# One 320-column maxima product, one shared output bank, centred weights, keys in three runs, and adds moved from GpSimd to VectorE

## The reference, cut to what matters

```python
x = x + layernorm(attention(layernorm(x)))
x = x + layernorm(ffn(layernorm(x)))
```

## Time and profile before

| | |
|---|---|
| median of 3 runs | 3582.44 us (3581.54 to 3588.01) |
| span of the profiled execution | 3584.1 us |
| what lies around the span in that execution | the page gives no time of its own beside the span; the span is 1.7 us above the median of the runs |
| TensorE matmuls | 3478.6 us busy (97%) |
| TensorE weight loads | 2683.5 us (75%) |
| VectorE | 2311.2 us (64%) |
| GpSimd | 2222.2 us (62%) |
| ScalarE | 1977.0 us (55%) |

### The profile page before, as it was taken

The page is one execution under the profiler, slowest core; times in us unless marked ns, Lnnn a source line. Parts: engine busy times, 40 slices in busy tenths (PEclk is TensorE's granted clock), DMA queues, the critical chain, the costliest instruction groups (busy, mean ns, idle before and its releaser), DMA issues.

```text
span 3584.1 us, 79850 instructions
## 1 busy us (share of the span) xinstructions
PE 3478.6 (97%) x29010; PEld 2683.5 (75%) x29010; DVE 2311.2 (64%) x4796; ACT 1977.0 (55%) x4132; POOL 2222.2 (62%) x3475
## 2 busy tenths in 40 slices
PE   8999999999997999999999999999999999999997
PEld 6888888888886677777777777777777777777774
DVE  5444444444434577777777777777777777777774
ACT  3222222222223567776676767777677767777674
POOL 1000000000001688889888898888988888988887
PEclk9999999999997899999999999999999999999999
DMA  6877887787777566666666666666666666666641
GB/s 176 240 224 210 228 235 221 209 236 229 216 236 172 131 147 155 147 150 155 150 152 147 153 152 151 150 148 155 154 150 146 151 153 157 149 144 151 153 117 42
DMA packets 493810, 603.94 MB, mean 169 GB/s; under 512 B 51080, under 2 KB 260120, under 8 KB 493480
## 3 DMA queue, kind: packets, MB, share of 16 engines
q1 hardware_dynamic: 413512, 564.80, 61.9%
q10 hardware_dynamic: 79680, 34.70, 5.4%
q0 software_dynamic: 288, 0.08, 0.0%
HBM read 361.59 MB, written 203.23 MB: 158 GB/s over the span
## 4 chain that ended last, share of the span: by engine, by line
PE 41%; POOL 17%; ACT 4%; issue 3%; ACTq 2%; DVE 1%; DMA 1%; POOLq 0%; SPq 0%; DVEq 0%
PE ps_misc L1118 11%; PE ps_sc L1049 5%; PE ps_ml L1025 4%; PE ps_mg L1030 4%; PE ps_o L1077 3%; PE ps_sc L1063 3%; PE ps_s L1096 3%; PE ps_o L1102 3%; POOL qk L809 3%; PE ps_s L1090 2%; POOL qk L812 2%; POOL qk L806 2%; ACTq L892 2%; POOL xb L842 2%; POOL ot_lo L827 2%
## 5 line engine op out<-in xcount | busy, mean ns | idle before, releaser
L937 DVE TENSOR_REDUCE mx<-ps_ml 128x2 f32<-128x384 f32 x1024 | 559.5, 546 | 334.5 <-PE ps_ml L1025 327.3
L499 PE MATMUL po<-ht_hi,w_both 128*128 128x512 f32 x2048 | 639.3, 391 | 1.6 <-ACT ht_hi L290 1.5
L897 ACT ACTIVATE ps_ml<-mask 128x384 f32<-128x384 bf16 x1022 | 500.1, 491 | 235.0 <-issue 116.2
L869 ACT ACTIVATE qk<-ps_sc 128x384 f32<-128x384 f32 (+1 forms) x1024 | 415.6, 458 | 210.6 <-PE ps_sc L1049 209.5
L499 PEld LDWEIGHTS po<-ht_hi,w_both 128*128 128x128 f32 x2048 | 385.2, 188 | 88.6 <-issue 6.5
L940 DVE TENSOR_REDUCE mx<-ps_mg 128x2 f32<-128x256 f32 x1024 | 424.7, 415 | 2.1 <-PE ps_mg L1030 1.9
L499 PE MATMUL po<-ht_lo,w_both 128*128 128x512 f32 x1024 | 399.0, 390 | 0.0
L882 ACT ACTIVATE v<-ps_sc 128x512 f32<-128x512 f32 x512 | 302.6, 592 | 93.7 <-PE ps_sc L1063 82.6
L806 POOL TENSOR_SCALAR_AFFINE_SELECT qk<-qk 128x512 f32<-128x512 f32 (+1 forms) x512 | 298.2, 582 | 87.6 <-ACT qk L869 85.0
L809 POOL TENSOR_SCALAR_AFFINE_SELECT qk<-qk 128x512 f32<-128x512 f32 x512 | 324.9, 635 | 35.0
L858 ACT ACTIVATE xb<-xb,nmb,rsb 128x512 f32<-128x512 f32 x384 | 310.4, 809 | 53.8 <-POOL nmb L799 53.5
(11 more groups left out here) (149 smaller groups left out, 8738.6 us busy)
## 6 DMA issues: line engine op xcount, KB each, us to landing
xb<-in_L_attn_x SPq DMA_DIRECT2D x256, 256.0 KB, 5.7
w_both<-q_hi_d SPq DMA_DIRECT2D x256, 256.0 KB
ks<-k_hi_d SPq DMA_DIRECT2D x128, 288.0 KB
q_lo_d<-o_lo SPq DMA_DIRECT2D x32, 1024.0 KB, 8.6
k_lo_d<-o_lo SPq DMA_DIRECT2D x32, 1024.0 KB, 10.1
w_both<-q_lo_d SPq DMA_DIRECT2D x128, 256.0 KB
vw<-v_d SPq DMA_DIRECT2D x128, 256.0 KB, 2.9
out<-xb SPq DMA_DIRECT2D x128, 256.0 KB, 3.3
```

The lines of the kernel that those rows point to most:

```text
L499: last = nc.tensor.matmul(po[bank(o, u)][:], wa[:, k, o * P:(o + 1) * P], ha[u][:, k, :], start=start, stop=stop)
L869: nc.scalar.activation(p_loc[:, i, 2 * hp:2 * hp + 2, lo:MW], ps_sc[n % 2][:, 0:2 * MW].rearrange("p (h n) -> p h n", h=2)[:, :, lo:MW], A ...
L897: nc.scalar.activation(ps_ml[u % 2][:, :, 0:MW], mask[:].rearrange("p (o n) -> p o n", o=1).to_broadcast([P, 2, MW]), ACT.Copy).then_inc(s ...
L937: nc.vector.tensor_reduce(mx[s % 2][:, 0, heads, tile], ps_ml[u % 2][:, :, 0:MW], axis=AX.X, op=ALU.max).then_inc(ml_taken, 1)
```

## The change

1. **Maxima.** Local and global keys of a tile are made neighbours in `ks`, so one product of 320 columns replaces the 192 and the 128. For this the local keys are kept in three runs with two copies of the global keys between them (`RUNS`, `GLOB_AT`); a window of 320 columns at `WINDOW_AT[tile]` holds both. The bank pair `ps_mx` is seeded with a 320-column mask (two layouts of it), and one VectorE reduction over blocks of 64 columns replaces two. A new piece `maxc` joins the blocks with three small VectorE instructions.
2. **Shared bank.** `ps_mx` takes four banks, so `ps_o` and `ps_s` become one, `ps_os`: the products with v (`ol`), the copy out (`oc`), the sums (`sl`, `sg`), their transpose, the global product (`pvgo`) and its scaling (`ogm`) use it one after another. The sums are made in four windows in one piece.
3. **Centred weights.** The mean over the output columns is taken out of `w_out`, of the second layer's matrix and of both biases, so the outputs of both layers have zero mean. Norm and residual add become one VectorE instruction, `x1` and `za`; the norm on ScalarE, the add on GpSimd and one small GpSimd instruction go.
4. **Adds.** The overlap adds go from GpSimd to VectorE (`sadd`).
5. **Loads.** Local keys come in three DMAs instead of one, global keys and values and the bias row only where they change. v is held in three buffers by step. The input of the next chunk is loaded right behind the store of the same tile. Scores and exponentials are separate pieces of the list, and all its offsets are new (`PERIOD` 16.5).

```diff
-KROW = SPAN + NGLOB
+RUNS = ((0, 2 * WIN, 0), (2 * WIN, 6 * WIN, 4 * WIN), (6 * WIN, 9 * WIN, 10 * WIN))
+GLOB_AT = (2 * WIN, 8 * WIN)
+TILE_AT = (0, 4 * WIN, 6 * WIN, 10 * WIN, 12 * WIN)
+KROW = SPAN + 2 * NGLOB
+WINDOW_AT = (0, 2 * WIN, 6 * WIN, 8 * WIN)
+MWG = P + WIN + NGLOB
...
-                for k in range(KT):
-                    dve.wait_ge(split_hi, k + 1)
-                    nc.vector.tensor_tensor(wo_lo[:, k, :], wo[:, k, :], wo_hi[:, k, :].bitcast(F32), ALU.subtract).then_inc(split_lo, 1)
+                dve.wait_ge(spec_loaded[1], 16)
+                nc.vector.tensor_reduce(wo_sum[:], wo[:], axis=AX.X, op=ALU.add).then_inc(wo_summed, 1)
...
+                    nc.vector.tensor_reduce(m_rows[:, a:a + 1], wi[:, a, :], axis=AX.X, op=ALU.add).then_inc(m_summed, 1)
...
     def load_ones(self, act, g):
...
+        for lo, hi, at in RUNS:
+            act.dma_start(ks[ROWS_MAX:ROWS_MAX + 1, :, at:at + hi - lo].bitcast(F32),
...
     def load(self, sp, c, g):
...
-            sp.dma_start(ks[dst, :, 0:SPAN].bitcast(F32),
-                         kd[rows, :].rearrange("(h p) n -> p h n", p=DH)[:, :, pad_at:pad_at + SPAN]).then_inc(done, 16)
-            sp.dma_start(ks[dst, :, SPAN:KROW].bitcast(F32),
-                         gd[rows, :].rearrange("(h p) n -> p h n", p=DH)[:, :, glob_at:glob_at + NGLOB]).then_inc(done, 16)
+            for lo, hi, at in RUNS:
+                sp.dma_start(ks[dst, :, at:at + hi - lo].bitcast(F32),
+                             kd[rows, :].rearrange("(h p) n -> p h n", p=DH)[:, :, pad_at + lo:pad_at + hi]).then_inc(done, 16)
+            if c % CPB == 0:
+                for at in GLOB_AT:
+                    sp.dma_start(ks[dst, :, at:at + NGLOB].bitcast(F32),
+                                 gd[rows, :].rearrange("(h p) n -> p h n", p=DH)[:, :, glob_at:glob_at + NGLOB]).then_inc(done, 16)
...
-        ps_ml = [pb(f"ps_ml{b}", [P, 2, 256]) for b in range(2)]
-        ps_mg = pb("ps_mg", [P, 4, P])
+        ps_mx = [pb(f"ps_mx{b}", [P, 2, 512]) for b in range(2)]
...
-        ps_o = pb("ps_o", [P, 512])
-        ps_s = pb("ps_s", [P, 512])
+        ps_os = pb("ps_os", [P, 512])
...
(TensorE, max)
-                            last = nc.tensor.matmul(ps_ml[u % 2][:, n, 0:MW], queries[n], keys[n][:, tile * P:tile * P + MW],
+                            last = nc.tensor.matmul(ps_mx[u % 2][:, n, 0:MWG],
+                                                    qs[g][0:ROWS_MAX, 2 * pair + n, tile * P:(tile + 1) * P],
+                                                    ks[g][0:ROWS_MAX, 2 * pair + n, WINDOW_AT[tile]:WINDOW_AT[tile] + MWG],
                                                     start=False, stop=True, skip_group_check=True)
-                            last = nc.tensor.matmul(ps_mg[:, n, :], queries[n], keys[n][:, SPAN:KROW], start=True, stop=True)
...
(VectorE)
+                        nc.vector.tensor_reduce(mb[s % 2][:, heads, tile, :],
+                                                ps_mx[u % 2][:, :, 0:MWG].rearrange("p h (b n) -> p h b n", n=WIN), axis=AX.X,
+                                                op=ALU.max).then_inc(mx_taken, 1)
...
+                    if name == "maxc":
...
+                        nc.vector.tensor_reduce(dst[:, 1, :, :], two(2, 3), axis=AX.X, op=ALU.max).then_inc(glob_joined, 1)
+                        nc.vector.tensor_reduce(dst[:, 0, :, :], two(0, 7), axis=AX.X, op=ALU.max).then_inc(pair_joined, 1)
+                        dve.wait_ge(pair_joined, s + 1)
+                        nc.vector.tensor_tensor(dst[:, 0, :, :], dst[:, 0, :, :], pairs[:, :, 4::5], ALU.max).then_inc(loc_joined, 1)
+                    if name == "sadd":
+                        dve.wait_ge(loc_masked, 4 * s + i + 2)
+                        nc.vector.tensor_tensor(p_sum[:, i, :, :], p_loc[:, i, :, P:MW], p_loc[:, i + 1, :, 0:WIN], ALU.add).then_inc(s_added, 1)
...
+                        nc.vector.scalar_tensor_tensor(xb[:, i, :], yb[:, i, :], rs[0][:, i:i + 1], xb[:, i, :],
+                                                       ALU.mult, ALU.add).then_inc(x1_done, 1)
...
(TensorE, sums)
+                    if name == "sl":
+                        pe.wait_ge(o_copied, s + 1)
+                        pe.wait_ge(s_added, 3 * s + 3)
...
+                        for n, (sums, windows) in enumerate(((halves[:, 0:3, 0, :], p_loc[:, 0:3, :, WIN:P]),
+                                                             (halves[:, 0:3, 1, :], p_sum[:]),
+                                                             (ps_os[:, CHUNK - P:CHUNK], p_loc[:, 3, :, WIN:MW]),
+                                                             (ps_os[:, CHUNK - WIN:CHUNK], p_last[:]))):
```

More of the change, by code:

```diff
@@ L18 @@
 from concourse import mybir
+from collections import defaultdict
 from contextlib import ExitStack
@@ new lines, in attention_phase @@
+        STEP = {
+            "max": (-24.199, -24.541, -18.13, -16.452, -14.377, -20.916, -12.047, -10.469),
+            "maxr": (-21.658, -24.356, -16.156, -17.544, -24.046, -13.821, -14.424, -11.914),
+            "seed": (-26.179, -17.313, -14.321, -21.944, -17.917, -12.257, -11.667, -5.155),
+            "maxc": (-11.643,),
+            "mt": (-8.224,),
+            "x_mt": (-6.202,),
+            "loc": (0.725, -0.098, 1.268, 5.513, 1.373, 4.656, 9.953, 10.057),
+            "x_loc": (-1.026, 6.374, 1.546, 2.758, 2.501, 12.223, 4.157, 8.885),
+            "locm": (-3.93, 0.616, -5.376, 4.294),
+            "sadd": (11.06, 10.318, 9.79),
+            "last": (4.706,),
+            "x_last": (6.509,),
+            "lastm": (-3.272,),
+            "glob": (6.095, 12.016, 7.262, 12.082),
+            "x_glob": (11.47, 10.271, 4.491, 8.982),
+            "ol": (12.531, 13.851, 13.964),
+            "oc": (12.4,),
+            "sl": (16.483,),
+            "sg": (17.734,),
+            "sums": (18.556,),
+            "pvgo": (22.001,),
+            "rglob": (20.077,),
+            "ogm": (24.906,),
+            "rloc": (20.57,),
+            "olm": (14.394,),
+            "osum": (20.265,),
+        }
@@ L734, in attention_phase @@
+            return [it[1:] for it in items]
+        SCORED = {"mt": "x_mt", "loc": "x_loc", "last": "x_last", "glob": "x_glob", "tr": "x_tr"}
         ORDER = timeline()
-        UNITS = [(*it, hp) for it in ORDER if it[0] in ("loc", "glob", "last", "mt", "tr") for hp in range(1 + (it[0] == "loc"))]
+        UNITS = [it for it in ORDER if it[0] in SCORED]
         UNIT_AT = {u: n for n, u in enumerate(UNITS)}
-        unit = lambda s, name, i, hp=0: UNIT_AT[name, s, i, hp]
-        LAST_USE = max((("loc", 3, 1), ("last", 0, 0), ("glob", 3, 0)), key=lambda use: unit(GROUPS, *use))
+        unit = lambda s, name, i: UNIT_AT[name, s, i]
@@ L739, in attention_phase @@
+        exps = iter((SCORED[name], s, i) for name, s, i in UNITS)
+        ORDER = [next(exps) if it[0] in SCORED.values() else it for it in ORDER]
+        LAST_USE = max((("loc", 7), ("last", 0), ("glob", 3)), key=lambda use: unit(GROUPS, *use))
         MISC = [it for it in ORDER if it[0] in ("out", "ffn") and it[2] % KT == 0]
@@ L1087, in item @@
-                        for n, (sums, windows) in enumerate(parts):
+                        for tile in O_PARTS[i]:
+                            if tile < 4:
+                                pe.wait_ge(loc_masked, 4 * s + tile + 1)
+                            else:
+                                pe.wait_ge(last_masked, s + 1)
+                            for h in range(4):
+                                rows, head = slice(h * DH, (h + 1) * DH), slice(h * DH, (h + 1) * DH)
+                                if tile < 4:
+                                    x0, w = (0, P) if tile == 0 else (P * tile - WIN, MW)
+                                    last = nc.tensor.matmul(ps_os[rows, x0:x0 + w], vw[s % V_BUFS][:, tile, head], p_loc[:, tile, h, MW - w:MW],
+                                                            start=tile == 0, stop=False, skip_group_check=True)
+                                else:
+                                    last = nc.tensor.matmul(ps_os[rows, CHUNK - WIN:CHUNK], vl[s % V_BUFS][:, head], p_last[:, h, :],
+                                                            start=False, stop=True, skip_group_check=True)
```

476 lines of the change are left out of this document (249 added, 227 removed).

## The result

The changed kernel takes 3468.3 us (median of 4 runs, 3463.28 to 3477.74) against 3582.5 before: the ratio is 0.9679 with a 95% interval of 0.9659 to 0.9699. Its profiled execution took 3463.28 us with a span of 3461.5, so 122.6 less than the span of the earlier trace rows. The forecast, which was worked out against the span, was 3444.

A forecast was written before the change was run, and what follows sets the result against it. TensorE was taken to bound the step, GpSimd a close second. From 3584.1 us, 121 steps x 1.2 = 145 saved, +8 at the border and -3 at the end gave 3444; whole range 3345 to 3565, likeliest case 3400 to 3490.

The forecast's parts named there:

- Maxima, -1.0: TensorE's maxima products: a unit falls from 0.47 to 0.34 us, eight units saving 1.0 us a step (0 to 1.4).
- Sums, -0.2: TensorE's sums: four windows at 1.13 us replace six at 1.32, saving 0.2 us a step (0 to 0.44).
- TensorE's waits for GpSimd, zero: TensorE waits 0.2 us a step for GpSimd's selects; change taken as zero, bounds minus 0.2 and plus 0.3.
- Rival 1: GpSimd was the real bound; the step falls to VectorE's limit, about 16.7 us, giving 3348 us; chance 0.17.
- VectorE, 16.3 to 16.8: VectorE's busy time a step rises from 14.12 to 16.3 to 16.8 us; bounds 15.9 and 18.4.
- The sentence on the rule: VectorE instructions reading two SBUF tiles contend with GpSimd's SBUF reads, the second waiting; at most 0.05 us each by rows.
- rival 3: VectorE becomes the bound through dear instructions or contention with GpSimd; step 19.2 us, kernel slower at 3652 us; chance 0.12.
- The 17.49: Forecast step in us: 18.69 less 1.0 for maxima and 0.2 for sums, above VectorE's 16.3 to 16.8.
- Rival 2: VectorE at 94% in fixed order delivers late and TensorE's banks wait; step about 18.1 us, 3519 us; chance 0.20.
- Shared bank and loads, nothing: The shared bank's chain, some 8 of 17.5 us a step, stays covered; DMA share 0.65 stays or falls; nothing added.
- rival 4: The shared bank holds TensorE: four hand-overs at 0.3 us eat the 1.2 us gain, giving 3589 us; chance 0.03.
- Border, +8: Between the blocks: later VectorE and ScalarE work, first seed about 2 us later, first maxima DMA 4; +8 us (0 to +25).

The follow-up runs named there:

- e3: Changed kernel with each 320-column maxima product split again into 192 and 128 columns, the one reduction kept: 3554.5 us, ratio 0.9911 to before.
- e9: Changed kernel with GpSimd's local scaling, sum with the global part and low part each replaced by two fills: 3406.2 us, ratio 0.9505 to before.
- e2: Changed kernel with one more VectorE reduction of 512 columns a tile, result unused: 3518.0 us, ratio 0.9812 to before.
- e6: Changed kernel with one more ScalarE copy of 384 columns a step into an unused tile: 3459.4 us, ratio 0.9654 to before.
- v1: Changed kernel with sums of squares on ScalarE replacing VectorE's statistics for the two outer norms: 3512.9 us, ratio 0.9807 to before.
- e1: Changed kernel with the three overlap adds a step back on GpSimd, behind each tile's second select: 3530.9 us, ratio 0.9852 to before.
- e5: Changed kernel with the last norm's fused VectorE instruction as a ScalarE scaling and a GpSimd addition: 3526.4 us, ratio 0.9849 to before.
- m1: Separate test without attention: VectorE repeats one instruction alone or beside GpSimd's; the fused one took 752 ns alone, 1633 beside additions.
- e4: Changed kernel with all large GpSimd instructions that read SBUF replaced by chains of short fills: 4029.3 us, ratio 1.1249 to before.
- e7: Changed kernel with only the first of three overlap adds on GpSimd, behind the second tile's selects: 3525.6 us, ratio 0.9837 to before.
- e8: Changed kernel with the first overlap add on GpSimd, but behind the last tile's selects: 3483.1 us, ratio 0.9715 to before.

## Why the prediction came out

The direction, the bound and the order of size were right: the result lies 24 us above the forecast, inside the range and inside the likeliest case's own range. It was put together from terms of which some were off against each other.

| term | forecast us | measured us |
|---|---|---|
| steps | -145 | -112.6 |
| border of the blocks | +8 | -5.9 |
| end | -3 | -4.1 |
| sum | -140 | -122.6 |

(Measured between three points of the two traces: VectorE's first transpose of the global reciprocals at 1171.5 and 1165.6 us, its last, 127 steps on, at 3530.7 and 3412.2, and the end of the span.)

The first seven steps, where no gain was counted, gave 2.9 us of the 112.6.

*The step before.* It was counted as 2000 / 107 = 18.69; the first and last start in the same row give 18.61. That is 0.08 of the 1.2 us forecast, some 10 us of the 145. The remedy was on the row itself.

*Maxima, -1.0.* The clean unit is 0.32 (forecast 0.34), and e3 shows that TensorE's work is passed on. But the starts of all products in the stretch, each to the next matmul, give 3.17 us of maxima a step for 3.72 before, so -0.55. A unit before was 0.47, as forecast; a unit after is 0.40 and not 0.34. The forecast compared a held and a clean unit before with a clean unit alone after. In e9 the maxima take 2.76, a unit 0.35: 0.96 less than before, which is the forecast's gain; so the price of the work was right, and what held the units went with three of GpSimd's reads or its shorter queue.

*Sums, -0.2.* 1.25 from start to start for 1.32, and 1.13 was forecast: measured gain 0.1.

*TensorE's waits for GpSimd, zero.* This was too little. The row was read as all that TensorE waited for GpSimd. The wait for the overlap adds (14.2 us, shown above) stood in the same view and was left out, so the direct waits were 36.7 us, 0.34 a step; in the changed kernel there are none. There are further gains outside the parts that the change edits: the products of `out` and `ffn` take 0.4 us a step less from start to start, those of the global keys 0.2 less, and those of `loc` 0.3 more, for they wait for exponentials. Most of the 0.4 is one gap a step before the products of `last`: their first came 564 ns after the start of the product before it, where such a product takes 240, and the waits name ScalarE's exponentials. The chain of before put 17% on GpSimd, and of after none, so part of this may be GpSimd's cost by way of other engines; no run shows how much. Rival 1 had seen GpSimd's share, and had given it 2 us a step instead of a few tenths.

*VectorE, 16.3 to 16.8.* It is 17.0. The reduction (0.804) was right. The five instructions with two SBUF inputs were put at 0.42 and 0.69 and took 0.66 and 0.95, 1.25 us more in all: the 1.1 of the contention, and 0.06 for each fused one, which takes 752 ns alone where the subtraction taken for it takes 688. The busy time rose by less, since the forecast's upper end had counted no overlap. This term is the weakest step of the prediction. It set the duration by rows from a stretch where GpSimd does nearly nothing. The sentence on the rule had the mechanism, and rival 3 nearly the price (1.5 us), but only as a way to slower; its sign, such instructions well over 0.75 us, came without its result.

*The 17.49.* e9 shows what lies behind it. With three of GpSimd's reads gone the step is 17.23 and TensorE has hardly a gap, so the sum for TensorE was sound, even a little high. Between 17.23 and 17.73 stand VectorE's contention with the waits that it makes, and the 1.0 us by which GpSimd's queue was shorter in e9; the runs don't part the two. Rival 2 (18.1) is true in its mechanism at some two fifths of its size, 0.24 us above the forecast step for 0.6: half of what VectorE has more comes through (e2), and its sign is there, since TensorE waits 49.9 us in 102 steps for VectorE's bias additions (40.3 at L1046, 9.6 at L1066), where it waited for none before.

*ScalarE and GpSimd.* 13.2 and 12.4 us, under the 14.2 and near the 11.9 of the forecast. A seed takes 704 ns (bound 0.82). e6 shows ScalarE's slack to be real for an instruction that adds no wait of its own. v1 shows that it isn't for one that waits.

*Shared bank and loads, nothing.* The waits of TensorE for the copy of the bank (`o_loc`) are 4.9 us in 102 steps, and the DMA share stayed at 0.65. By these waits rival 4 is out.

*Border, +8.* The work behind the last product and the ones rows did come 2.4 us later, as forecast. That the first maxima's DMA would take 4 us more was wrong: it took 5.4 less. The runs don't show why; the DMA share there did not fall (0.66 before and 0.81 after, 1120 to 1180 us).

*What the parts are worth.* Taken back one at a time, the wide products cost 86 us (e3), the adds 62 (e1) and the fused last norm 58 (e5). That is 206 of a gain of 114, so these are not shares of it: each part was taken out of a list whose offsets were laid for all of them. No run takes back the shared bank, the loads or the new offsets by themselves, and how much of the gain is theirs stays open.

*Weight loads as the measure.* The Trainium skill, Perfetto Trace Analysis, section "Identifying the Most-Contended Engine", takes the weight loads' share of the time, beside the share of the peak operation rate, as the good measure for TensorE. Here that share is 71% of the steps (1276 of 1800 us), and still e3's extra products came through, so for this kernel the matmuls' time from start to start was the better guide.

## What to carry to other kernels

Before a VectorE instruction that reads two SBUF tiles is priced, look at what GpSimd does in the stretch where it will run: in this kernel's steps it cost a sixth to over a half more (883 and 1021 ns for 752, 664 for 424), and in m1, where GpSimd added without a break, it took 2.2 to 3.2 times as long as alone. GpSimd is slowed too. Where a few engines work down fixed lists at over 70% each, price a move by the waits at its new place and not by the load that it takes away: one add of 0.7 us cost 57 us at one place and 15 at another, and three moves that took 0.7 to 1.4 us a step off VectorE gained nothing. Read a period from the first and last start, and read the chain's engine shares for what an engine costs by way of others.

## What the runs showed of the hardware

- Sharing between VectorE and GpSimd costs both (m1): fused instruction 752 to 1633 ns and addition on GpSimd 1262 to 1590 beside one another; fused 752 to 979 and select 612 to 946; addition of 256 columns on VectorE 424 to 1366 beside GpSimd's additions. I had expected one to wait for the other, the other unharmed. Beside fills the fused instruction stays at 752, and the fill takes 524 ns, as in e4.
- A tiny instruction with two SBUF inputs varies as well: the maximum of two 16-element tiles took 346 ns in the changed kernel, 522 in e7 and 313 in e8, where GpSimd's add stands at different places. That this is the sharing was not measured by itself.
- Splitting a reduction of 640 elements into ten blocks of 64 costs nothing beyond its elements: 804 ns, for 0.81 worked out from those of two blocks.
- A sum of squares with its running sum on ScalarE comes as two instructions, 626 ns for 512 columns and 190 ns for reading the sum:

```profile
L988 ACT ACTIVATION_READ_ACCUMULATOR junk<-xb 128x1 f32 x199 | 37.8, 190 | 0.0
```
